# Issuing the first loads of a hybrid attention and mixture kernel from SyncE, and taking a maximum over partitions on TensorE and VectorE

## The chip, the cores and the metric

The kernel runs on one core of one Trainium2 chip. The metric is the device time of one execution in microseconds; lower is better. The engines are named PE (TensorE), DVE (VectorE), ACT (ScalarE), POOL (GpSimd) and SP (SyncE).

## The reference

The input x has the shape [2, 2048, 256], 4096 tokens of 256 float32 values, and passes four residual blocks: linear attention, a mixture-of-experts FFN, causal softmax attention, and the same FFN again.

```python
x = x + attn_a(_layernorm(x), Wqkv, Wout, bout)
x = x + ffn(_layernorm(x), ln_gamma, ..., gens, gc_w, gc_b)
x = x + attn_b(_layernorm(x), Wq, bq, Wk, bk, Wv, bv, Wo, bo)
x = x + ffn(_layernorm(x), ln_gamma, ..., gens, gc_w, gc_b)
```

In the FFN the output of the experts is multiplied by three matrix exponentials before it is mixed with a dense branch:

```python
for i in range(NROT):                  # NROT = 3
    moe_out = moe_out @ expm(gens[i])  # gens: [3, 256, 256]
```

Only weights go into the exponentials, so the kernel computes them once, before it touches x, and folds their product into the experts' second weights.

## The kernel before, in words

`build` calls five stages one after the other: `weights()`, `context()` (linear attention), `mixture(0)`, `attention()` and `mixture(1)`. A stage is one block, in which each engine has its own instruction stream; streams meet only through semaphores, and at the end of a block all engines meet at a barrier. The order on each engine is the order in which the code is written.

The change lies in `weights()`, L185 to L536, which works on three matrices of 256x256 in float32 (NROT = 3, each as two chunks of 128 partitions):

- **ScalarE** (L407) first issues the load of the generators (L409, semaphore `w_gens`), then the four projection matrices of the softmax attention (L411), x in four pieces of 1 MB (L414), and the small weights of the linear attention (L416 to L419). Only then comes its compute: the copies of PE's transposes out of the PSUM banks (L422, recorded as L163, since the helper `copy` stands there).
- **SyncE** (L226) issues 14 small loads (L241 to L245, semaphore `w_small`), waits for `w_gens`, and issues the experts' weights: `ew1` in two pieces of 2 MB (L248) and `ew2` in four of 1 MB (L251). Last it writes a blank tile (L255).
- **GpSimd** (L258) builds constants (iotas, identity, masks, zeros), then waits for `g_mx` and takes the maximum over all 128 partitions with `partition_all_reduce` (L306, semaphore `g_all`).
- **VectorE** (L308) sums the absolute values of each generator row (L338), takes the maximum per partition (L340, signals `g_mx`), waits for `g_all`, works out from the maximum how many squarings are needed and the scale (L342 to L348), and scales the generators (L350, signals `A_ok`).
- **TensorE** (L448) waits for the identity and for `A_ok`, transposes each scaled matrix (L454, inside the helper `transposed`), and forms powers of it with `product` (L462) from the transposes that ScalarE has copied. VectorE copies the squares out (L355), builds polynomials (L359, L362), and finishes Horner's scheme (L377). A hardware loop then squares the results (L384), two products join the three exponentials (L387, L389), and the stage ends with small products that need the experts' weights (L508, which waits for `w_ew`) and the projections (L516, `w_proj`), and with splits into bfloat16 parts on VectorE (L322 to L327).

`context()` starts behind the barrier. There SP issues nothing at first, GpSimd fills a row with ones (L648) and then takes inverse square roots with the operation `pow` for each group of tokens (L579, in `roots`), VectorE takes statistics of x (L561 to L572), waits for the root, and normalises (L680); PE's first work in this stage is the transpose of the first normalised group (L788), and all its other work of the stage stands behind it.

Of the kernel before, what the change touches and what calls it, by code (L numbers as in the profile page):

```python
# [18 lines left out]
ACT, ALU, AX = mybir.ActivationFunctionType, mybir.AluOpType, mybir.AxisListType  # L19
P = 128  # L20
# [5 lines left out]
def build(nc, d, out):  # L26
    B, N, C = d["L0_attn_a_x"].shape
    HD = d["L0_attn_a_Wout"].shape[0]
# [5 lines left out]
    NT = T // P  # L34
# [13 lines left out]
    with ctx:  # L48
# [5 lines left out]
        def sem(name):  # L54
            taken.append(nc.alloc_semaphore(name))
            return taken[-1]
# [15 lines left out]
        xs = sb("xs", [P, NT, C])  # L72
        keys = under("keys", [P, 2, KC, N], F32)
        rows = under("rows", [P, 2, 2, (KC + HC) * P], F32)
# [19 lines left out]
        ident = sb("ident", [P, P])  # L94
# [74 lines left out]
        def weights():  # L169
# [23 lines left out]
            gsum = a2.take(NROT * KC)  # L193
            gmx, gall = a2.take(1), a2.take(1)
            thr = a2.take(24)
# [12 lines left out]
            dve = sem("dve_order")  # L208
            g_mx, g_all, A_ok, AT_ps, AT_ok = sem("g_mx"), sem("g_all"), sem("A_ok"), sem("AT_ps"), sem("AT_ok")
            horner_ps, X_ok, s_ok = sem("horner_ps"), sem("X_ok"), sem("s_ok")  # L210
# [14 lines left out]
            with nc.Block() as block:  # L225
                @block.sync  # L226
                def _(sp):
# [17 lines left out]
                    sp.dma_start(gcb[:], d["L0_ffn_gc_b"].partition_broadcast(P)).then_inc(w_small, 16)  # L245
                    sp.wait_ge(w_gens, 16)
                    for c in range(KC):
                        sp.dma_start(ew1[:, c, :, :], d["L0_ffn_ew1"][:, c * P:(c + 1) * P, :].rearrange("e p h -> p e h")  # L248
                                     ).then_inc(w_ew, 16)
# [9 lines left out]
                def _(pool):  # L259
                    n = 0  # L260

                    def then(ins):
                        nonlocal n
                        n += 1
                        ins.then_inc(order, 1)
                        pool.wait_ge(order, n)

                    def select(t, pattern, base, cm, op, fill):
                        return pool.affine_select(out=t, in_=t, compare_op=op, fill=fill, base=base, pattern=pattern,
                                                  channel_multiplier=cm)  # L270
# [8 lines left out]
                    then(pool.memset(ident[:], 0.0))  # L279
                    select(ident[:], [[-1, P]], 0, 1, ALU.not_equal, 1.0).then_inc(consts, 1)  # L280
                    then(pool.memset(eye, 0.0))
                    select(eye, [[P, KC], [-1, C]], 0, 1, ALU.not_equal, 1.0).then_inc(consts, 1)
# [16 lines left out]
                    pool.memset(onesb[:], 1.0).then_inc(consts, 1)  # L299
                    pool.memset(onesf[:], 1.0).then_inc(consts, 1)  # L300
                    pool.memset(mhalf[:], -0.5).then_inc(consts, 1)
                    for t in (eb1p, eb2p, abbp, vbp):
                        pool.memset(t[:], 0.0).then_inc(consts, 1)

                    pool.wait_ge(g_mx, 1)
                    pool.partition_all_reduce(gall, gmx, P, bass.bass_isa.ReduceOp.max).then_inc(g_all, 1)  # L306

                @block.vector  # L308
                def _(v):
                    n = 0  # L310

                    def then(ins):

                        nonlocal n
                        n += 1
                        ins.then_inc(dve, 1)
                        v.wait_ge(dve, n)

                    def parts(o, src, width, rows):
# [19 lines left out]
                                         apply_absolute_value=True))  # L339
                    v.tensor_reduce(gmx, gsum, AX.X, ALU.max).then_inc(g_mx, 1)  # L340
                    v.wait_ge(g_all, 1)
                    then(v.tensor_scalar(cmp, thr, gall, None, ALU.is_lt))  # L342
                    then(v.tensor_reduce(sf, cmp, AX.X, ALU.add))
# [7 lines left out]
                    v.wait_ge(A_ok, NROT)  # L351
                    v.wait_ge(consts, 2)
                    for m in range(NROT):
# [54 lines left out]
                def _(act):  # L408
                    act.dma_start(gens, d["L0_ffn_gens"].rearrange("m (c p) j -> p m c j", p=P)).then_inc(w_gens, 16)  # L409
                    for o, k in zip(w4, "qkvo"):  # L410
                        act.dma_start(o, d[f"L0_attn_b_W{k}"].rearrange("(c p) n -> p c n", p=P)).then_inc(w_proj, 16)  # L411
                    for q in range(4):
                        ts = slice(q * NT // 4, (q + 1) * NT // 4)
                        act.dma_start(xs[:, ts, :], d["L0_attn_a_x"].rearrange("b (n p) c -> p (b n) c", p=P)[:, ts, :]  # L414
                                      ).then_inc(x_in, 16)
                    act.dma_start(wqkv, d["L0_attn_a_Wqkv"].rearrange("(c p) n -> p c n", p=P)).then_inc(x_in, 16)  # L416
                    act.dma_start(wout[:], d["L0_attn_a_Wout"]).then_inc(x_in, 16)
                    for b in range(B):
                        act.dma_start(ctxm[HD:HD + 1, b, :], d["L0_attn_a_bout"].rearrange("(o n) -> o n", o=1)).then_inc(x_in, 16)  # L419
                    for m in range(NROT):  # L420
# [28 lines left out]
                def _(pe):  # L449
# [15 lines left out]

                    pe.wait_ge(consts, 1)
                    for m in range(NROT):
# [1267 lines left out]
```

## Time and profile before

| what | value |
|---|---|
| median of 3 runs | 1540.83 us (1539.09 to 1541.23) |
| the profiled execution | 1532.49 us |
| its span, first to last instruction | 1530.9 us |
| mean granted TensorE clock | 0.885 of full speed |
| busy share PE / DVE / ACT / POOL | 78% / 50% / 37% / 27% |
| `weights()`, to the first instruction of `context()` | 0 to 140.1 us |

A row of the timeline gives the start in us from the start of the span, the duration, the engine, the line, the operation, what is written and read, and the count where equal instructions were merged; in brackets stands the idle time of the engine ahead of it and what ended that time. ACTq, SPq and POOLq are the engines' instruction queues, where DMA issues and configuration instructions are recorded. "issue" as a releaser means that the engine waited for nothing that the profile shows. Clock is a share of full speed: 1.00 is 2.4 GHz and 0.50 is 1.2 GHz.

### The profile page before, as it was taken

What the parts mean: (1) busy time and instruction counts of PE and PEld (TensorE: products, weight loads), DVE (VectorE), ACT (ScalarE), POOL (GpSimd) and SP (SyncE); (2) the same over time, 40 slices, a digit from 0 to 9 for tenths busy, and PEclk for the clock granted to TensorE, in tenths of its full rate; (3) what the DMA queues carried; (4) which work ended last, traced back from release to release, by engine and by line L of the source; (5) the groups of instructions that cost most, each with busy time, mean ns of one, the idle gap of its engine ahead of it and who ended that gap; (6) DMA issues with size and microseconds to landing.
All of it is one profiled execution on the core that took longest, in us unless ns stands there. A gap on an engine that the chain in (4) does not pass through costs nothing. (4 is left out here: it accounts for less than half of the span.)

```text
span 1530.9 us, 26055 instructions
## 1 busy us (share of the span) xinstructions
PE 1200.2 (78%) x7496; PEld 1008.5 (66%) x7497; DVE 761.7 (50%) x2430; ACT 573.2 (37%) x1143; POOL 412.3 (27%) x479
## 2 busy tenths in 40 slices
PE   1895886991899999930789968998881899999940
PEld 1772664871788888830679856897770778888830
DVE  1624674885334444448644455444775234444438
ACT  0110553440444444445333223332440344444435
POOL 2001110477243443410100010000576244443410
PEclk8998897696899999975899989999785999999975
DMA  9200233267633333343000000000266743333346
GB/s 317 86 0 0 83 124 124 90 204 231 221 120 98 100 94 96 97 164 109 1 0 1 1 1 0 1 1 1 111 221 230 250 136 96 122 98 93 97 170 220
DMA packets 75432, 161.12 MB, mean 105 GB/s; under 512 B 11270, under 2 KB 36562, under 8 KB 75354
## 3 DMA queue, kind: packets, MB, share of 16 engines
q1 hardware_dynamic: 49190, 99.42, 18.8%
q0 software_dynamic: 19776, 54.45, 11.6%
q10 hardware_dynamic: 6388, 6.29, 1.3%
q8 instruction: 38, 0.62, 0.2%
q14 instruction: 40, 0.33, 0.1%
HBM read 88.66 MB, written 71.47 MB: 105 GB/s over the span
## 5 line engine op out<-in xcount | busy, mean ns | idle before, releaser
L1397 PE MATMUL bank<-ew,rows 128*128 x852 | 298.5, 350 | 5.9 <-DVE rows L1076 3.0
L1399 PE MATMUL bank<-ew,rows 128*128 x852 | 274.1, 322 | 0.0
L1398 PE MATMUL bank<-low_in,rows 128*128 x852 | 273.7, 321 | 0.0
L1189 POOL DMA_INDIRECT results<-xh x142 | 141.8, 999 | 353.5 <-DVE xh L1059 209.6
L1076 DVE TENSOR_TENSOR rows<-bank,rows 128x512 fp32r<-128x512 f32 x142 | 98.3, 692 | 217.8 <-ACT rows L163 217.8
L1397 PEld LDWEIGHTS bank<-ew,rows 128*128 128x128 f32 x852 | 162.2, 190 | 14.9 <-issue 8.0
L1399 PEld LDWEIGHTS bank<-ew,rows 128*128 128x128 f32 x852 | 162.7, 191 | 12.6
L1398 PEld LDWEIGHTS bank<-low_in,rows 128*128 128x128 f32 x852 | 163.6, 192 | 6.8
L163 ACT ACTIVATE rows<-bank 128x256 fp32r<-128x256 f32 (+1 forms) x284 | 138.8, 489 | 69.1 <-PE bank L1405 66.9
L579 POOL TENSOR_TENSOR work<-work,mhalf 128x8 f32<-128x8 f32 (+1 forms) x20 | 37.9, 1894 | 450.5 <-DVE work L572 450.4
L163 ACT ACTIVATE xh<-bank 128x256 f32<-128x256 f32 (+1 forms) x181 | 76.4, 430 | 196.1 <-PE bank L1431 139.1
L1282 ACT ACTIVATE xh<-bank 128x512 f32<-128x512 f32 x142 | 84.9, 598 | 153.2 <-PE bank L1416 153.2
L1169 POOL DMA_INDIRECT slots_in<-xh,work x128 | 126.9, 992 | 51.4 <-issue 36.0
L1052 DVE TENSOR_TENSOR rows<-bank,rows 128x256 fp32r<-128x256 f32 x142 | 60.3, 425 | 153.9 <-ACT rows L163 153.0
L1330 PE MATMUL bank<-abw,work 128*128 128x256 f32 (+1 forms) x512 | 113.0, 356 | 4.4 <-ACT ab L1264 2.4
L1613 PE MATMUL bank<-values,shares 128*128 128x256 f32 x816 | 111.8, 288 | 2.0 <-DVE shares L1541 1.9
L1613 PE MATMUL bank<-keys,queries 128*128 128x512 f32 (+2 forms) x480 | 107.9, 379 | 4.8 <-issue 4.8
L1405 PE MATMUL bank<-ident,xh 128*128 128x128 f32 x284 | 56.1, 279 | 69.1 <-DMA xh<-slots_in 68.9
L1613 PEld LDWEIGHTS bank<-values,shares 128*128 128x128 f32 x816 | 101.3, 190 | 3.5 <-DVE shares L1541 3.2
L1330 PEld LDWEIGHTS bank<-abw,work 128*128 128x128 f32 x512 | 88.5, 222 | 21.0 <-ACT ab L1264 5.1
L1613 PEld LDWEIGHTS bank<-keys,queries 128*128 128x128 f32 x480 | 86.2, 197 | 18.5 <-issue 5.2
L1405 PEld LDWEIGHTS bank<-ident,xh 128*128 128x128 f32 x284 | 40.1, 145 | 81.5 <-issue 63.2
(285 smaller groups left out, 2068.6 us busy)
## 6 DMA issues: line engine op xcount, KB each, us to landing
xh<-slots_in POOLq DMA_DIRECT2D x142, 129.0 KB, 2.5
xh<-results SPq DMA_DIRECT2D x16, 1032.0 KB, 5.5
low_in<-low SPq DMA_DIRECT2D x32, 512.0 KB, 4.5
residual<-xs SPq DMA_DIRECT2D x16, 512.0 KB, 5.8
dense<-ab SPq DMA_DIRECT2D x16, 512.0 KB, 5.8
xs<-residual SPq DMA_DIRECT2D x16, 512.0 KB, 4.5
ab<-dense SPq DMA_DIRECT2D x16, 512.0 KB, 5.4
xs<-in_L_attn_a_x_dram ACTq DMA_DIRECT2D x4, 1024.0 KB
```

The costliest lines, as they stand in the source:

```text
L163: return eng.activation(o, i, ACT.Copy, scale=scale)
L1052: v.tensor_tensor(f32r(q[:, 1]), bank[:, k % 2, 0:C], q[:, 0], ALU.subtract).then_inc(xrT_ok, 1)
L1076: v.tensor_tensor(f32r(q[:, 1]), bank[:, 4 + k % 2, :], q[:, 0], ALU.subtract).then_inc(hidT_ok, 1)
L1169: pool.indirect_dma_start(out=xg, out_offset=bass.IndirectOffsetOnAxis(ap=slot[:, k, t:t + 1], axis=0), in_=xh[:, t, :], in_offset=None).t ...
L1189: pool.indirect_dma_start(out=yg, out_offset=bass.IndirectOffsetOnAxis(ap=back[j % RING], axis=0), in_=yr[j % RING], in_offset=None).then_ ...
L1282: act.activation(hid[k % 2], bank[:, 2 + k % 2, :], ACT.Gelu).then_inc(hid_ok, 1)
L1330: pe.matmul(o, xT[g % 2][:, c, t * P:(t + 1) * P], abw[:, c, some], start=(c == 0), stop=False)
L1397: pe.matmul(o, hi, f32r(high(c)), start=(c == 0), stop=False)
L1398: pe.matmul(o, hi, f32r(low(c)), start=False, stop=False)
L1399: pe.matmul(o, lo, f32r(high(c)), start=False, stop=False)
L1405: last = pe.transpose(bank[:, k % 2, c * P:(c + 1) * P], xr[k % RING][:, c * P:(c + 1) * P], ident[:])
L1613: last = pe.matmul(o, f32r(left(x)), f32r(right(y)), start=(start and q == 0), stop=(stop and q == 2), skip_group_check=True)
```

## The change

ScalarE keeps only the load of the generators. The loads of x, of the small weights of the linear attention and of the four projections move to SyncE, in this order, between its wait for `w_gens` and the loads of the experts' weights. The maximum over partitions goes another way: PE transposes the column of 128 partial maxima into one row of PSUM bank 7, VectorE reduces that row, PE multiplies a row of ones with the result so that it stands in all 128 partitions, and VectorE copies it out. GpSimd writes the row of ones (`onesf`) earlier, right behind the identity, and no longer runs `partition_all_reduce`.

```diff
 @block.sync
     sp.wait_ge(w_gens, 16)
+    for q in range(4):
+        ts = slice(q * NT // 4, (q + 1) * NT // 4)
+        sp.dma_start(xs[:, ts, :], d["L0_attn_a_x"].rearrange("b (n p) c -> p (b n) c", p=P)[:, ts, :]
+                     ).then_inc(x_in, 16)
+    sp.dma_start(wqkv, d["L0_attn_a_Wqkv"].rearrange("(c p) n -> p c n", p=P)).then_inc(x_in, 16)
+    sp.dma_start(wout[:], d["L0_attn_a_Wout"]).then_inc(x_in, 16)
+    for b in range(B):
+        sp.dma_start(ctxm[HD:HD + 1, b, :], d["L0_attn_a_bout"].rearrange("(o n) -> o n", o=1)).then_inc(x_in, 16)
+    for o, k in zip(w4, "qkvo"):
+        sp.dma_start(o, d[f"L0_attn_b_W{k}"].rearrange("(c p) n -> p c n", p=P)).then_inc(w_proj, 16)
     for c in range(KC):
         sp.dma_start(ew1[:, c, :, :], ...
 @block.gpsimd
     select(ident[:], [[-1, P]], 0, 1, ALU.not_equal, 1.0).then_inc(consts, 1)
+    pool.memset(onesf[:], 1.0).then_inc(consts, 1)
...
     pool.memset(onesb[:], 1.0).then_inc(consts, 1)
-    pool.memset(onesf[:], 1.0).then_inc(consts, 1)
...
-    pool.wait_ge(g_mx, 1)
-    pool.partition_all_reduce(gall, gmx, P, bass.bass_isa.ReduceOp.max).then_inc(g_all, 1)
 @block.vector
     v.tensor_reduce(gmx, gsum, AX.X, ALU.max).then_inc(g_mx, 1)
+    v.wait_ge(g_row, 1)
+    v.tensor_reduce(gtop, bank[0:1, 7, 0:P], AX.X, ALU.max).then_inc(g_top, 1)
     v.wait_ge(g_all, 1)
+    then(v.tensor_copy(gall, bank[:, 7, P:P + 1]))
     then(v.tensor_scalar(cmp, thr, gall, None, ALU.is_lt))
...
-    v.wait_ge(consts, 2)
+    v.wait_ge(consts, 3)
 @block.scalar
     act.dma_start(gens, d["L0_ffn_gens"].rearrange("m (c p) j -> p m c j", p=P)).then_inc(w_gens, 16)
-    for o, k in zip(w4, "qkvo"):
-        act.dma_start(o, d[f"L0_attn_b_W{k}"].rearrange("(c p) n -> p c n", p=P)).then_inc(w_proj, 16)
-    for q in range(4):
...
-    act.dma_start(wqkv, d["L0_attn_a_Wqkv"].rearrange("(c p) n -> p c n", p=P)).then_inc(x_in, 16)
-    act.dma_start(wout[:], d["L0_attn_a_Wout"]).then_inc(x_in, 16)
...
 @block.tensor
-    pe.wait_ge(consts, 1)
+    pe.wait_ge(consts, 2)
+    pe.wait_ge(g_mx, 1)
+    pe.transpose(bank[0:1, 7, 0:P], gmx, ident[:]).then_inc(g_row, 1)
+    pe.wait_ge(g_top, 1)
+    pe.matmul(bank[:, 7, P:P + 1], onesf[:], gtop, start=True, stop=True).then_inc(g_all, 1)
     for m in range(NROT):
         pe.wait_ge(A_ok, m + 1)
```

How the instructions of GpSimd stand before, from the end of `weights()` over the start of `context()`. The rows "ISA" without a tile are recorded in the trace as MODIFY_POOL_CONFIG, the row "ISA work<-work" is the reduction over partitions, and the TENSOR_TENSOR rows of L579 are the `pow`:

```order
L303 MEMSET vbp 65x256
L306 ISA
L306 ISA work<-work 128x1 [waits g_mx]
L225 UNCONDITIONAL_BRANCH
L646 UNCONDITIONAL_BRANCH [waits barrier_Pool_Activation_PE_DVE_SP_gather]
L648 MEMSET work 1x4096
L579 ISA
L579 TENSOR_TENSOR ab<-ab,mhalf 128x8 [waits a_arg,a_ones]
L579 TENSOR_TENSOR ab<-ab,mhalf 128x8 [waits a_arg] x7
```

The same place of the change, where the line numbers are higher by 4 in `context()`:

```order
L650 UNCONDITIONAL_BRANCH [waits barrier_Pool_Activation_PE_DVE_SP_gather]
L652 MEMSET work 1x4096
L583 TENSOR_TENSOR ab<-ab,mhalf 128x8 [waits a_arg,a_ones]
L583 TENSOR_TENSOR ab<-ab,mhalf 128x8 [waits a_arg] x7
L630 UNCONDITIONAL_BRANCH
```

The reduction has gone with the configuration instruction ahead of it, and so has the configuration instruction ahead of the first `pow`. One at the program's start (L272, now L282) remains.

SyncE in the change, from its wait for the generators to its last store of the stage:

```order
L249 DMA xs<-in_L_attn_a_x_dram 128x8x256 [waits w_gens]
L249 DMA xs<-in_L_attn_a_x_dram 128x8x256 x3
L251 DMA ab<-in_L_attn_a_Wqkv_dram 128x2x192
L252 DMA wout<-in_L_attn_a_Wout_dram 64x256
L254 DMA ctxm<-in_L_attn_a_bout_dram 1x256 x2
L256 DMA ab<-in_L_attn_b_Wq_dram 128x2x256
L256 DMA ab<-in_L_attn_b_Wk_dram 128x2x256
L256 DMA ab<-in_L_attn_b_Wv_dram 128x2x256
L256 DMA ab<-in_L_attn_b_Wo_dram 128x2x256
L258 DMA ew<-in_L_ffn_ew_dram 128x8x512 x2
L261 DMA ew<-in_L_ffn_ew_dram 128x8x256 x4
L265 DMA slots_in<-zero 128x258 [waits zero_ok]
```

Before, the wait for `w_gens` stood directly at the loads of `ew`; now twelve loads stand between. On ScalarE this is what remains ahead of its copies:

```order
L417 UNCONDITIONAL_BRANCH [waits barrier_Pool_Activation_PE_DVE_SP_release]
L419 DMA xh<-in_L_ffn_gens_dram 128x6x256
L163 ACT_TABLE_LOAD
L163 ACTIVATE xh<-bank 128x512 [waits AT_ps] x3
L163 ACTIVATE ab<-bank 128x512 [waits A3_ps] x3
```

The table load stands directly behind the one DMA, and only the copy behind it waits for PE.

## Rows read from the trace of the kernel before

**Rows 1.** Page, first line.

```profile
span 1530.9 us, 26055 instructions
```

**Rows 2.** Timeline from 0 us: the path from the generators to ScalarE's first copies.

```profile
6.22 1.75 DVE L338 TENSOR_REDUCE work<-xh 128x6 f32<-128x1536 f32 x1 [2.99 <-DMA xh<-in_L_ffn_gens_dram]
...
8.01 0.16 DVE L340 TENSOR_REDUCE work<-work 128x1 f32<-128x6 f32 x1
...
18.91 12.05 ACTq L416 DMA_DIRECT2D ab<-in_L_attn_a_Wqkv_dram  x1
20.13 0.38 POOL L306 PARTITION_ALL_REDUCE work<-work  x1 [6.96 <-issue]
20.55 0.24 DVE L342 TENSOR_SCALAR work<-work 128x24 f32<-128x24 f32 x1 [12.38 <-POOL work L306]
...
22.48 2.79 PE L454 MATMUL bank<-ident,xh 128*128 128x128 f32 x12 [22.48 <-DVE xh L350]
...
33.39 1.28 ACT L163 ACT_TABLE_LOAD   x1 [33.39 <-issue]
34.68 1.57 ACT L163 ACTIVATE xh<-bank 128x512 f32<-128x512 f32 x3
...
39.25 0.69 DVE L355 COPY xh<-bank 128x512 f32<-128x512 f32 x1 [16.12 <-PE bank L462]
40.89 0.69 DVE L355 COPY xh<-bank 128x512 f32<-128x512 f32 x1 [0.95 <-PE bank L462]
```

**Rows 3.** Timeline of PE alone, the first products.

```profile
35.33 12.43 PE L462 MATMUL bank<-xh 128*128 128x256 f32 x48 [10.06 <-ACT xh L163]
```

**Rows 4.** Configuration instructions of GpSimd, lines L306 and L579.

```profile
L306 POOLq MODIFY_POOL_CONFIG  x2: 1/1/1, 13.1 to 13.2; - x2
L579 POOLq MODIFY_POOL_CONFIG  x2: 1/1/1, 143.7 to 143.7; - x2
```

**Rows 5.** Timeline at the start of `context()`.

```profile
140.13 3.50 POOL L648 MEMSET work<- 1x4096 f32 x1 [119.62 <-POOLq L225]
...
142.42 1.25 DVE L572 TENSOR_SCALAR ab<-ab 128x4 f32<-128x4 f32 x1
150.46 1.68 POOL L579 TENSOR_TENSOR ab<-ab,mhalf 128x8 f32<-128x8 f32 x1 [6.82 <-issue]
```

**Rows 6.** Single lines, durations in ns (min/median/max): the nearest to the four new instructions.

```profile
L454 PE MATMUL bank<-ident,xh x12: 421/422/447, 22.5 to 24.9; 128*128 128x128 f32 x12
L524 PE MATMUL bank<-work,ab x8: 250/250/272, 133.4 to 134.2; 128*128 128x1 f32 x8
L697 DVE TENSOR_REDUCE ab<-bank x8: 411/418/426, 169.7 to 244.5; 128x32 f32<-128x256 f32 x8
L402 DVE TENSOR_SCALAR qbias<-bank x1: 159/159/159, 137.1 to 137.1; 128x2 f32<-128x2 f32 x1
```

**Rows 7.** Windows: us, busy PE PEld DVE ACT POOL (instructions), clock, DMA share, GB/s.

```profile
38.00:39.00 1.00, 1.00 (x4) 0.76 (x3) 0.00 (x0) 0.00 (x0) 0.00 (x0) 0.50 1.10 344
39.00:40.00 1.00, 1.00 (x6) 0.90 (x5) 0.69 (x1) 0.00 (x0) 0.00 (x0) 0.99 1.11 330
...
59.00:60.00 1.00, 0.90 (x3) 0.82 (x4) 1.00 (x2) 0.00 (x0) 0.00 (x0) 0.75 0.39 132
...
60.00:100.00 40.00, 40.00 (x206) 34.84 (x206) 12.60 (x19) 8.00 (x15) 0.00 (x0) 0.96 0.00 0
```

**Rows 8.** Timeline: SyncE's loads of the experts' weights, and PE's first use.

```profile
8.30 2.60 SPq L248 DMA_DIRECT2D ew<-in_L_ffn_ew_dram  x2
...
10.93 28.25 SPq L251 DMA_DIRECT2D ew<-in_L_ffn_ew_dram  x4
...
112.67 13.90 PE L508 MATMUL bank<-ew,work 128*8 128x512 f32 x32
```

**Rows 9.** DMA issues: size of each, and median us from issue to landing.

```profile
xh<-in_L_ffn_gens_dram ACTq DMA_DIRECT2D x1, 768.0 KB, 5.2
...
ab<-in_L_attn_b_Wo_dram ACTq DMA_DIRECT2D x1, 256.0 KB, 9.0
```

More of the change, by code:

```diff
@@ L193, in weights @@
             gsum = a2.take(NROT * KC)
-            gmx, gall = a2.take(1), a2.take(1)
+            gmx, gall, gtop = a2.take(1), a2.take(1), a2.take(1, rows=1)
             thr = a2.take(24)
@@ L208, in weights @@
             dve = sem("dve_order")
-            g_mx, g_all, A_ok, AT_ps, AT_ok = sem("g_mx"), sem("g_all"), sem("A_ok"), sem("AT_ps"), sem("AT_ok")
+            g_mx, g_row, g_top, g_all, A_ok, AT_ps, AT_ok = sem("g_mx"), sem("g_row"), sem("g_top"), sem("g_all"), sem("A_ok"), sem("AT_ps"), sem("AT_ok")
             horner_ps, X_ok, s_ok = sem("horner_ps"), sem("X_ok"), sem("s_ok")
@@ L409, in _ @@
                     act.dma_start(gens, d["L0_ffn_gens"].rearrange("m (c p) j -> p m c j", p=P)).then_inc(w_gens, 16)
-                    for o, k in zip(w4, "qkvo"):
-                        act.dma_start(o, d[f"L0_attn_b_W{k}"].rearrange("(c p) n -> p c n", p=P)).then_inc(w_proj, 16)
-                    for q in range(4):
-                        ts = slice(q * NT // 4, (q + 1) * NT // 4)
-                        act.dma_start(xs[:, ts, :], d["L0_attn_a_x"].rearrange("b (n p) c -> p (b n) c", p=P)[:, ts, :]
-                                      ).then_inc(x_in, 16)
-                    act.dma_start(wqkv, d["L0_attn_a_Wqkv"].rearrange("(c p) n -> p c n", p=P)).then_inc(x_in, 16)
-                    act.dma_start(wout[:], d["L0_attn_a_Wout"]).then_inc(x_in, 16)
-                    for b in range(B):
-                        act.dma_start(ctxm[HD:HD + 1, b, :], d["L0_attn_a_bout"].rearrange("(o n) -> o n", o=1)).then_inc(x_in, 16)
                     for m in range(NROT):
```

## The prediction

> **What bounds the kernel now.** I read the page first, then the timeline of the first 140 us, then the windows for the clock and the DMAs. The span is 1530.9 us [rows 1], and the change touches only `weights()`. It matters there because every stage ends at a barrier: what `weights()` takes is added to all that follows, whatever the engines' shares of busy time are.
>
> The reader is to see three waits. The first is on GpSimd. VectorE has its partial maxima at 8.17 us (8.01 + 0.16), but the reduction over partitions starts only at 20.13, after 6.96 us in which GpSimd waits for nothing the profile shows, and VectorE goes on at 20.55, after 12.38 us of idleness [rows 2]. The configuration instruction for that reduction stands at 13.1 to 13.2 [rows 4], so the order is: masks until 13.17, configuration, 6.96 us, 0.38 us of work.
>
> The second is on ScalarE. PE transposes the three matrices from 22.48 to 25.27 [rows 2], then idles for 10.06 us until ScalarE has copied the first one [rows 3]. ScalarE did not wait for PE: its queue was issuing loads until 33.39 (the one of the Wqkv weights alone held it for 12.05 us), and only then come the table load of 1.28 us and the first copy at 34.68 [rows 2]. The engines' DMA share is above 1.0 there and they move 330 to 344 GB/s [rows 7], so the issues are held up by full queues, and ScalarE's compute stands behind them.
>
> The third is in the next stage. GpSimd's fill ends at 143.63 and VectorE's argument is ready at 143.67 (142.42 + 1.25), yet the first `pow` starts at 150.46, after 6.82 us of "issue" [rows 5]. A configuration instruction stands at 143.7 here too [rows 4]. Since PE's first transposes of `context()` wait for this root, all of the stage waits with it.
>
> **Part 1, the maximum over partitions.** Removed: everything between 8.17 and 20.55, 12.38 us. Added: four small instructions in a chain with a handover between any two.
> - PE's transpose of one column, 128 columns moving: 0.42 us, as the first transposes of the stage took, which ran on a cold PE [rows 6].
> - VectorE's maximum of 1x128 from PSUM: no row has the shape. A 128x256 reduction from PSUM took 0.42, a 128x2 operation from PSUM 0.16 [rows 6]; half way in size, I take 0.30.
> - PE's product with one column: 0.25 from the products of 128x1 [rows 6]; doubled at half clock it would be 0.50.
> - VectorE's copy of 128x1 from PSUM: 0.16 from the 128x2 operation [rows 6].
> - Four handovers and one wait of VectorE for itself, at 0.04 each as between 20.13 + 0.38 and 20.55 [rows 2]: 0.20.
>
> Together 1.33 us, so L342 starts at 9.50 instead of 20.55: **11.05 us** earlier. The longest handover in these rows to PE is the 0.64 us from the start of L350, 21.84, to PE's start, and that holds an instruction of 0.43; two steps on PE that were each worse by 0.6 would cost 1.2, and I keep 9.8 as the low end. The row of ones is early enough: behind the identity its fill is done before 4 us, and the second matrix of constants is still waited for, by a count of three now, far ahead of its use.
>
> **A rule that speaks against this part.** The row shows 0.38 us for the reduction on GpSimd, less than my 1.33 us for the detour [rows 2]. The Trainium skill, GPSIMD Engine Reference, section "4.1 Engine selection", gives GPSIMD as the engine for a reduction along the partition dimension; by that rule alone the sum of this part would be a loss of 0.95 us, that is 1.33 less 0.38. The same page, "2.1 Instruction dispatch", says that the first call of a freshly loaded kernel pays about 6 us more with no visible instruction; the trace agrees, with 6.96 and 6.82 us.
>
> **Part 2, ScalarE freed.** With one DMA ahead, the table load runs from about 1.5 us, in the shadow of the generators' load. PE's transposes then run from 22.48 - 11.05 = 11.43 to 14.22 at the old pace. The first is done after a third of the 2.79 us, at 12.36, and ScalarE's first copy, about 0.6 us, ends at 13.0, before PE has finished transposing. So PE goes straight into its products at 14.22: the idle 10.06 us are gone, **10.06 us**, and nothing replaces them.
>
> **Part 3, the clock.** The first product of eight matmuls took from 35.33 to 39.2, the next 1.64 us (39.25 to 40.89) [rows 2, 3]. Clock was 0.50 until 39.0 and 1.00 from there [rows 7]; PE had then worked for 3.7 us, coming from idleness. In the change PE works unbroken from 11.43. If the clock rises 3.7 us from there, at 15.1, the first product has 0.9 us at half pace and ends 2.2 us after its start, not 3.9: a gain of 1.7. If it rises 3.7 us behind the products' start, the gain is 0. I take **1.0 us**.
>
> **Part 4, the generators' load.** Alone on ScalarE's queue it no longer shares the DMA engines with four projections. It took 5.2 us for 768 KB [rows 9]; at 330 GB/s [rows 7] the bytes alone are 2.4 us of that, and a fixed part that no row gives apart is the rest. Three of the four shared loads were issued by the time its bytes flowed, so I bound the gain by 0 and 0.7 and take **0.3 us**.
>
> **Part 5, the next stage.** The change has no configuration instruction left ahead of `pow`, only the one at the program's start. With it goes the wait: `pow` starts when the argument is ready, 143.7 instead of 150.46 in old time: **6.75 us**. This edit is in no line of the diff; it follows from the order of instructions on GpSimd.
>
> **What moves at no cost.** Twelve more loads on SyncE stand behind its wait for the generators. That wait costs nothing new: the small issues keep SyncE busy until 8.3 [rows 8], later than the generators land (6.2). Behind it come 13.9 MB (x 4096 KB, Wqkv, wout and projections 1280, `ew1` and `ew2` 8192). After 33.4 us ScalarE issues nothing, and the engines still move 330 to 344 GB/s from SyncE's queue [rows 7], so one queue fills them. At 330 the last byte lands at 8.3 + 42 = 50 us. The experts' weights are first used at 112.67 [rows 8], or 90 in the change: 40 us of cover. The biases and norm weights on SyncE's queue are wanted by VectorE after 58 us, now after 35; they are issued as before by 8.3, and the slowest of the loads beside them took 9.0 us [rows 9]. x is wanted at 117 at the earliest. The blank tile of SyncE, ahead of the barrier, is issued behind the last load, by about 46, also long before the barrier. If this cover were gone, each us by which the weights came after 90 would be lost.
>
> Behind the first products the chain of PE, VectorE and ScalarE moves as a whole: from 60 to 100 us PE was busy all 40 us with no DMA at all [rows 7]. One term may change: around 59.5 us, in the gap before PE's start at 59.1, the clock fell (0.75 over 59 to 60), and its mean of 0.96 from 60 to 100 says that it stayed at 0.50 for 3.2 us of those 40 [rows 7], at a cost of about 1.7 us. Whether it falls again when all stands 22 us earlier, and when it rises at the start of `context()`, is open: between -2 and +2 us, taken as 0.
>
> **Sum.** 11.05 + 10.06 + 1.0 + 0.3 + 6.75 = 29.2 us. The profiled execution took 1532.49 us, 1.6 beyond its span, and would take 1503.3. The median of the runs is 1540.83, 8.3 above the profiled one; I see no reason for the gain to scale and subtract it from the median: **1511.7 us**.
>
> **Rivals.**
> - *`pow` still waits for its code* at its first use, since what the start of the program configured is not resident by then. For it: 6.82 us are seen at that place, and no row shows a `pow` without a change of configuration ahead of it. Against: both waits follow such an instruction, and iotas and masks run at once at the start. Gain 22.4, time 1518.4. Chance 12%.
> - *One queue feeds the engines less well than two*, and PE waits for the experts' weights. At 330 GB/s there is no wait; at 140, the 13.9 MB take 99 us and end at 107.6, which is 17.5 too late: gain 11.7, time 1529. The Trainium skill, Perfetto Trace Analysis, "DMA Optimizations", advises balancing DMAs over the engines that can issue them where descriptor generation is the bottleneck, which speaks for this rival; the rows speak against its condition. Chance 2%.
> - *The same mechanism, slower than before*: it decides from below 125 GB/s, where the loads end after 8.3 + 111 = 119.4, the old 112.67 plus the 6.75 of part 5. At 110 GB/s they end at 134.7, 15.2 us past that: 1556. The nearest rows are three times faster. Chance 1%.
> - *ScalarE is not what PE waits for*: if the copies needed a first-use wait of their own of some 10 us, part 2 would fall and the gain be 19, time 1522. The table load in the rows is followed at once by the copy. Chance 3%.
>
> **How the numbers follow.** The forecast's case has 82%. Its own range adds the ends: at best 11.05 + 10.06 + 1.7 + 0.7 + 6.75 + 2 = 32.3, time 1508.5, and 1.5 more if the timed runs scatter as before (1539.1 to 1541.2); at worst 9.8 + 10.06 + 0 + 0 + 6.75 - 2 = 24.6, time 1516.2. The first rival lies at 1518.4 and is to be held for the most part, so the range is 1507 to 1520. A change under 0.2%, 3 us, could not be told from none here: faster 0.98, same 0.01, slower 0.01.
>
> **What would show it.** Right: L352 (the old L342) near 9.5 us, ScalarE's first copy near 12.4 and no idle time of PE ahead of L462; the first `pow` directly behind the fill of 4096 ones; the barrier of `weights()` near 118 us; DMAs finished by 55 us. Wrong: an "issue" wait of 6 us or more ahead of the first `pow` (the first rival), idle time of PE on a DMA ahead of L512 (the queue rivals), or a table load that starts late. The prediction fails as a whole if later stages, which have no edit, run longer by what was won.

## The result, and the profile after

| what | before | the change |
|---|---|---|
| median of 4 runs | 1541.03 us (1539.09 to 1542.66) | 1514.57 us (1512.38 to 1517.63) |
| the profiled execution | 1532.49 us | 1512.38 us |
| its span | 1530.9 us | 1510.8 us |
| first instruction of `context()` | 140.13 us | 119.47 us |
| first `pow` | 150.46 us | 123.19 us |

The ratio is 0.9847 (95% interval 0.9822 to 0.9871): the change is 26.5 us faster by the medians, where 29.2 were forecast. At the first `pow` it is 27.3 us ahead, at the first slot load of `mixture(0)` (the load of a tile of sorted tokens) 25.7, at the end of the profiled pair only 20.1; what is given back has a part of its own below.

The path to ScalarE's first copies, in the timeline of the change. Its columns are those explained ahead of the prediction, and the rows answer to [rows 2, 3]:

```profile
1.49 1.28 ACT L163 ACT_TABLE_LOAD   x1 [1.49 <-PEq L1728]
...
6.34 1.75 DVE L345 TENSOR_REDUCE work<-xh 128x6 f32<-128x1536 f32 x1 [3.22 <-DMA xh<-in_L_ffn_gens_dram]
...
6.92 3.55 POOL L279 TENSOR_SCALAR_AFFINE_SELECT sel<-sel 72x1024 bf16<-72x1024 bf16 x3
...
8.43 0.37 PE L468 MATMUL bank<-ident,work 128*1 128x128 f32 x1 [8.43 <-DVE work L347]
8.84 0.28 DVE L349 TENSOR_REDUCE work<-bank 1x1 f32<-1x128 f32 x1 [0.56 <-PE bank L468]
...
9.17 0.58 PE L470 MATMUL bank<-work,onesf 1*128 1x1 f32 x2 [0.37 <-DVE work L349]
9.79 0.16 DVE L351 COPY work<-bank 128x1 f32<-128x1 f32 x1 [0.68 <-PE bank L470]
9.99 0.52 DVE L352 TENSOR_SCALAR work<-work 128x24 f32<-128x24 f32 x1
...
11.56 1.92 DVE L360 TENSOR_SCALAR xh<-xh,work 128x512 f32<-128x512 f32 x3
...
12.47 2.82 PE L454 MATMUL bank<-ident,xh 128*128 128x128 f32 x12 [2.72 <-DVE xh L360]
...
15.09 12.01 PE L462 MATMUL bank<-xh 128*128 128x256 f32 x48
...
18.60 0.69 DVE L365 COPY xh<-bank 128x512 f32<-128x512 f32 x1 [5.11 <-PE bank L462]
```

The table load lies at the start, the four new instructions take the place of the reduction, and there is no bracket behind PE's products at 15.09: PE does not wait for ScalarE any more. The first copy out of the products stood at 39.25 before and stands at 18.60 now, 20.65 us earlier, and the whole stage keeps that: `context()` starts 20.66 us earlier. The start of `context()` on GpSimd, which answers to [rows 5]:

```profile
119.47 3.50 POOL L652 MEMSET work<- 1x4096 f32 x1 [105.74 <-POOLq L225]
...
121.69 1.32 DVE L575 TENSOR_SCALAR ab<-ab 128x4 f32<-128x4 f32 x1
121.77 1.25 DVE L576 TENSOR_SCALAR ab<-ab 128x4 f32<-128x4 f32 x1
123.19 1.67 POOL L583 TENSOR_TENSOR ab<-ab,mhalf 128x8 f32<-128x8 f32 x1 [0.21 <-DVE ab L576]
```

The `pow` now waits 0.21 us for VectorE instead of 6.82 us for nothing visible. VectorE's two TENSOR_SCALAR rows ahead of it end with GpSimd's fill, as the last section takes up. One queue feeds the DMA engines: in windows of 5 us of the change (columns as in [rows 7]) they move 334 to 387 GB/s from 15 us until the loads are done at about 50 us, 42 us ahead of the first use of the experts' weights at 92.01.

```profile
30.00:35.00 5.00, 3.72 (x18) 2.93 (x16) 5.00 (x9) 0.00 (x0) 0.00 (x0) 1.00 1.05 387
...
45.00:50.00 5.00, 5.00 (x25) 4.41 (x24) 2.08 (x3) 0.00 (x0) 0.00 (x0) 1.00 1.04 334
50.00:55.00 5.00, 5.00 (x30) 4.39 (x29) 1.38 (x2) 1.60 (x3) 0.00 (x0) 1.00 0.06 19
```

### The profile page after: what moved, and what is told of

Read it like the earlier page. It is cut to its first block and busy times, and to the rows that moved or that the text cites. A ratio compares the mean times of both kernels' runs of the same rounds, so it can differ in the third digit from the quotient of the medians.

```text
span 1510.8 us, 26058 instructions
## 1 busy us (share of the span) xinstructions
PE 1204.3 (80%) x7499; PEld 1010.8 (67%) x7500; DVE 763.9 (51%) x2432; ACT 573.7 (38%) x1143; POOL 412.8 (27%) x478
```

## The experiments

Theory: three waits went, two of them in series on one path (GpSimd's reduction, then ScalarE's queue of issues) and one in the next stage (the configuration ahead of `pow`). Rivals: ScalarE was not what PE waited for; `pow` waits at its first use whatever stands ahead; and what the profiled pair gives back later belongs to the loads on SyncE's queue. The diffs below are taken against the change.

**The kernel before once more.** No edit; a second profile.

> The kernel before, unchanged, for a second profile. In the first pair of profiles the change was 27.3 us ahead at the first pow of context(), still 25.7 at the first slot load of mixture(0), and only 20.4 at the end of that mixture. Theory A (scatter): the start of the expert tiles in mixture(0), where slot loads, scatters and low weights share the DMA engines, varies from run to run by about 5 us whatever the kernel; this second profile of before then has the same weights() (first instruction of context() at 140.1, first pow at 150.5, within 0.3) and reaches the first gather of results later than the first profile did, since the runs of before have a median 8 us over that profile: span about 1535 to 1540. Theory B (given back by a mechanism of the change): the profile of before repeats to 1 us, span about 1531, and the difference in mixture(0) belongs to the change.

Measured: 1540.45 us, ratio 1.0001 (0.9984 to 1.0017), span 1537.8. `context()` starts at 140.9 and the first slot load of `mixture(0)` stands at 383.6, as in the first profile within 1 us, but the span is 7 us longer. So the first profile of before was a short execution, and a difference of two spans is known to no better than that. What is called the stretch from here on, from the first slot load to the last scatter of results in `mixture(0)`, took 286.6 us (285.4 in the first profile). That is not the cause of the difference, so this did not decide between A and B. The wait of GpSimd ahead of the reduction was 5.95 us here, 6.96 in the first profile.

**The loads alone.** The maximum is taken on GpSimd again; the loads are where the change has them.

```diff
 @block.gpsimd
+    pool.wait_ge(g_mx, 1)
+    pool.partition_all_reduce(gall, gmx, P, bass.bass_isa.ReduceOp.max).then_inc(g_all, 1)
 @block.vector
-    v.wait_ge(g_row, 1)
-    v.tensor_reduce(gtop, bank[0:1, 7, 0:P], AX.X, ALU.max).then_inc(g_top, 1)
     v.wait_ge(g_all, 1)
-    then(v.tensor_copy(gall, bank[:, 7, P:P + 1]))
 @block.tensor
-    pe.wait_ge(g_mx, 1)
-    pe.transpose(bank[0:1, 7, 0:P], gmx, ident[:]).then_inc(g_row, 1)
-    pe.wait_ge(g_top, 1)
-    pe.matmul(bank[:, 7, P:P + 1], onesf[:], gtop, start=True, stop=True).then_inc(g_all, 1)
```

> The change of the loads alone; the maximum is taken on GpSimd as before. Own theory: the reduction still starts at about 20.1 behind 7 us of loading code, PE's transposes at about 22.5, and its products follow at 25.1 without idle time: weights() ends at about 129.5 to 130 instead of 140.1, and the first pow still waits 6.8 us behind the fill. Time 10 to 11 us below before, about 1530.5. Rival (ScalarE was not what PE waited for): PE idles ahead of its products as before, no gain. Rival (the clock makes up the difference): since PE's idle time is gone, the first product takes 2.2 instead of 3.9 us, and the gain is 11.8.

Measured: 1529.49 us, ratio 0.9928 (0.9911 to 0.9945), 11.1 us faster by the ratio. The timeline of this kernel, the same path, and its first `pow`:

```profile
19.25 0.38 POOL L316 PARTITION_ALL_REDUCE work<-work  x1 [6.06 <-issue]
...
21.59 2.79 PE L454 MATMUL bank<-ident,xh 128*128 128x128 f32 x12 [21.59 <-DVE xh L360]
...
24.18 11.41 PE L462 MATMUL bank<-xh 128*128 128x256 f32 x48
...
27.09 0.69 DVE L365 COPY xh<-bank 128x512 f32<-128x512 f32 x1 [4.85 <-PE bank L462]
```

```profile
127.71 3.50 POOL L648 MEMSET work<- 1x4096 f32 x1 [108.09 <-POOLq L225]
138.32 1.68 POOL L579 TENSOR_TENSOR ab<-ab,mhalf 128x8 f32<-128x8 f32 x1 [7.10 <-issue]
```

PE goes straight from its transposes into its products, as the theory has it, and `context()` starts 12.4 us earlier: 0.9 from a shorter wait of GpSimd (6.06 us), 10.3 from the idle time, 1.0 from the first product, which took 2.9 us instead of 3.9. The expectation was 10 to 10.6; the shorter wait, which varies as much between profiles of before, and the product make up the rest. The rival that ScalarE was not what PE waited for falls. `pow` waits 7.10 us here.

**The maximum alone.** ScalarE issues all its loads ahead of its copies, as before.

```diff
 @block.scalar
     act.dma_start(gens, ...).then_inc(w_gens, 16)
+    for o, k in zip(w4, "qkvo"):
+        act.dma_start(o, ...).then_inc(w_proj, 16)
...
 @block.sync
     sp.wait_ge(w_gens, 16)
-    for q in range(4):
-        ts = slice(q * NT // 4, (q + 1) * NT // 4)
...
```

> The change of the maximum alone; ScalarE issues all its loads as before. Own theory: PE's transposes are done by 16, but the first copy still stands at 34.7, so weights() ends at 140.1 as before; only the wait ahead of the first pow is gone, 6.6 us. Time about 1534.5. Rival (pow waits at its first use whatever stands ahead of it, and in the change something else hid this): no gain, 1541. Together with the loads alone this says that the two edits are not additive: each alone gives 10 to 11 and 0 in weights(), both give 20.6.

Measured: 1534.84 us, ratio 0.9964 (0.9951 to 0.9977), 5.5 us faster by the ratio. In its timeline PE is ready 10 us earlier and waits 10 us longer:

```profile
12.48 2.82 PE L454 MATMUL bank<-ident,xh 128*128 128x128 f32 x12 [2.98 <-DVE xh L350]
...
34.89 5.29 PE L462 MATMUL bank<-xh 128*128 128x256 f32 x15 [19.59 <-ACT xh L163]
...
139.68 3.50 POOL L652 MEMSET work<- 1x4096 f32 x1 [125.94 <-POOLq L225]
143.39 1.67 POOL L583 TENSOR_TENSOR ab<-ab,mhalf 128x8 f32<-128x8 f32 x1 [0.21 <-DVE ab L576]
```

`weights()` ends 0.4 us earlier, less than the 1.5 us by which the three profiles of before differ there (139.4 to 140.9), so nothing is to be told from that. The gain is the wait ahead of `pow`, gone with the configuration instruction. So in `weights()` the loads alone give 12.4 us, the maximum alone 0.4, and both 20.7: the second wait hid the first.

**A reduction that nobody reads.** The change, with the reduction beside the path, into a tile of its own.

```diff
 @block.gpsimd
+    pool.wait_ge(g_mx, 1)
+    pool.partition_all_reduce(gidle, gmx, P, bass.bass_isa.ReduceOp.max)
```

> The whole change, with partition_all_reduce put back on GpSimd beside it, its result going into a tile that nobody reads. Own theory: the reduction is off the path and costs nothing in weights() (context() starts at 119.5), but a configuration instruction stands ahead of the first pow again, and pow waits 6.8 us: 6.6 us slower than the change, about 1521. Rival (the wait has to do with the long path before, not with the change of configuration): as the change, 1514.6.

Measured: 1520.59 us, ratio 0.9869 (0.9846 to 0.9891): by the medians 6.0 us slower than the change, as expected, by the ratios 3.4, and their intervals overlap. The trace decides. The start of `context()` and the configuration in this kernel:

```profile
119.41 3.50 POOL L656 MEMSET work<- 1x4096 f32 x1 [98.86 <-POOLq L226]
129.96 1.68 POOL L587 TENSOR_TENSOR ab<-ab,mhalf 128x8 f32<-128x8 f32 x1 [7.05 <-issue]
```

```profile
L587 POOLq MODIFY_POOL_CONFIG  x2: 1/1/1, 122.9 to 123.0; - x2
```

`context()` starts as in the change (119.41), and the first `pow` 6.77 us later than there. In the code nothing else differs, so the wait belongs to the reduction and the configuration instruction that it leaves ahead of `pow`; the two were not taken apart. Using one `partition_all_reduce` costs 6 to 7 us twice, ahead of it (5.95 to 6.96 us in the five profiles with it) and ahead of the next `pow` (6.82 to 7.10). The rival that `pow` waits at its first use whatever stands ahead falls.

**The change once more.** No edit.

> The change, unchanged, for a second profile. In the profiles so far, the stretch from the first slot load of mixture(0) to its last scatter of results took 285.4 and 286.6 us in before, 287.9 with the maximum alone, but 289.7 in the change, 291.0 with the loads alone and 290.8 with the unused reduction: the three kernels with the loads on SyncE lose 3 to 5 us there, nearly all of it within the first seven tiles (43.0 to 43.8 against 47.0 to 47.8 us to the eighth scatter). Theory B (belongs to the loads on SyncE's queue): 289.5 to 291 again, 47 to 48 to the eighth scatter. Theory A (scatter of runs, three against three by chance): 285 to 291, anywhere.

This chip gave longer times for every kernel, the kernel before included (1577.42 us): from the first scatter of slots to the first slot load the change took 116.2 us here and 97.2 in its first profile. In `mixture(0)` PE waited 19.6 us for ScalarE's gelu (1.1 in the first profile), in the whole execution 42.3 us (2.4). The ratio to before is 0.9829 (0.9805 to 0.9853), 26.7 us by the medians. The stretch took 287.4 us, with 43.9 to the seventh scatter, the one that the expectation counts as the eighth: against theory B, on this chip.

**The loads late on ScalarE.** The change, with the moved loads back on ScalarE, behind its copies of the powers.

```diff
 @block.scalar
         act.wait_ge(A3T_ps, m + 1)
         copy(act, AT[:, m], ...).then_inc(A3T_ok, 1)
+    for o, k in zip(w4, "qkvo"):
+        act.dma_start(o, ...).then_inc(w_proj, 16)
...
```

> The change, but the moved loads go back to ScalarE's queue, behind its nine copies of the powers instead of ahead of them, so SyncE's queue carries what it did before. Theory B (the state or filling of SyncE's queue is what slows the first tiles of mixture(0)): that stretch is back to 285 to 288 us, 43 to 44 us to the eighth scatter, while context() still starts at 119.5: 3 to 4 us faster than the change, about 1511. Theory A (scatter): no difference to the change but for chance, 1514.6. If the late issue holds ScalarE back at the squaring (its next copy is at 51.2, its copies end at 29.2, and 5.5 MB are 16 us at 340 GB/s behind SyncE's 8.4 MB), context() starts later by what it overruns, at most a few us.

Measured on the same chip as the run above: 1552.20 us, ratio 0.9840 (0.9815 to 0.9866); `context()` starts at 120.0, the stretch took 287.1 us. No difference to the change can be told, in time or in the stretch, where theory B expected 3 to 4 us. That also shows that what helped is *when* ScalarE issues, not which engine does: with 5.5 MB on its queue behind the copies nothing is lost that these runs could show.

**Horner's scheme interleaved.** In the change one wait of PE is left in this part (timeline of PE of the change):

```profile
28.28 5.44 PE L462 MATMUL bank<-xh 128*128 128x256 f32 x24
38.44 11.85 PE L462 MATMUL bank<-xh 128*128 128x256 f32 x46 [4.72 <-DVE xh L387]
```

```diff
-for q, i in enumerate((3, 2, 1, 0)):
-    (both steps of polynomial i, for all m)
+poly(0, 3)
+for q, i in enumerate((2, 1, 0)):
+    poly(q + 1, i)
     v.wait_ge(b_ok, NROT * (q + 1))
     for m in range(NROT):
         v.wait_ge(horner_ps, NROT * q + m + 1)
         v.scalar_tensor_tensor(X[:, m], ...).then_inc(X_ok, 1)
```

> The change, with VectorE's polynomials built one at a time between the steps of Horner's scheme instead of all four ahead of them. In the change PE waits 4.7 us for VectorE at 38.4 and then runs 48 products, some of them at half clock. Own theory: the path through the first stage was handed to VectorE's polynomials (14.5 us) when ScalarE and GpSimd went off it; interleaved, PE has products to do meanwhile, its wait shrinks to about 1 us at a time and the clock does not fall: context() starts 5 to 6 us earlier, at about 114; time about 1509. Rival (VectorE and PE now alternate and each step waits for the other): no gain, 1514.6.

Measured on the same chip as the two above: 1544.38 us, ratio 0.9789 (0.9762 to 0.9815), 6.3 us below the change there. PE works without a gap, and the windows from 36 to 44 us show clock 1.00 throughout:

```profile
27.93 16.07 PE L464 MATMUL bank<-xh 128*128 128x256 f32 x72
44.03 1.85 PE L456 MATMUL bank<-ident,xh 128*128 128x128 f32 x12
```

`context()` starts at 113.2 instead of 119.3: 6.1 us.

**Before and the change on one chip.** No edits; these two and the two below ran on a third chip.

> The kernel before, for one more profile beside the next one on the same chip. Question: does the stretch of mixture(0) from the first slot load to the last scatter belong to the kernel or to chance? So far before: 285.4, 286.6 (first chip or chips). Theory A (chance, or the chip): this one and the next lie within 285 to 291 with no order between them. Theory B (the loads on SyncE slow it): this one is 3 us or more below the next.

> The change, for one more profile. Its stretch was 289.7 in the first profile and 287.4 in the second, on another chip. Theory A: no order against before on the same chip; with that the difference of the spans comes to what the first two stages win, 27.3 us, give or take the scatter of 3 to 5 us. Theory B: 3 us or more above before, and the difference of the spans is 20 to 24.

Measured: before 1538.54 us (beside 1540.42 for its other runs, ratio 0.9991), the change 1510.93 us, ratio 0.9805 (0.9772 to 0.9838), 29.5 us by the medians (27.6 against the run beside it). In this pair of profiles the change is 26.3 us ahead at the first `pow` (123.70 against 150.00) and 24.8 by the spans. The stretch took 287.0 and 286.7 us: no order between them.

**The fills moved.** The change, with two fills of GpSimd behind VectorE's urgent work.

```diff
 @block.gpsimd (weights)
+    pool.wait_ge(A_ok, NROT)
     pool.memset(onesb[:], 1.0).then_inc(consts, 1)
 @block.gpsimd (context)
-    pool.memset(work[HD:HD + 1, 0:T], 1.0).then_inc(ones_ok, 1)
-    pool.wait_ge(ones_ok, 1)
     for g in range(NG):
         nrm.roots(pool, g)
+    pool.wait_ge(nrm.root_ok, NG)
+    pool.memset(work[HD:HD + 1, 0:T], 1.0).then_inc(ones_ok, 1)
+    pool.wait_ge(ones_ok, 1)
```

> The change, with GpSimd's last six constants of weights() held back until the generators are scaled, and its fill of 4096 ones in context() behind all roots. In the change VectorE's three scalings took 1.92 us beside those fills and 1.28 before, and the arguments of the first pow took 1.3 us beside the fill of ones. Theory (the two engines hinder each other): scalings 1.28 again; from the start of context() to the first pow 2.6 instead of 3.7 us, 1.3 us in all, which the runs can hardly tell. Against it: the fill at the end lies ahead of the barrier; it ends before the stage does if the last root is taken 3.5 us before the end, as it was. Rival (those durations have another cause): no change in them.

Measured: 1513.25 us, ratio 0.9830 (0.9800 to 0.9860), no faster than the change. Its timeline at three places, and the times in ns of the four instructions of L686 near 193 us (least, median, most):

```profile
10.34 0.24 DVE L353 TENSOR_SCALAR work<-work 128x24 f32<-128x24 f32 x1
...
11.64 1.28 DVE L361 TENSOR_SCALAR xh<-xh,work 128x512 f32<-128x512 f32 x3
```

```profile
122.15 1.68 POOL L584 TENSOR_TENSOR ab<-ab,mhalf 128x8 f32<-128x8 f32 x1 [107.63 <-DVE ab L577]
```

```profile
192.73 0.16 DVE L681 SCALAR_TENSOR_TENSOR ab<-ab 128x4 f32<-128x4 f32 x1 [1.75 <-POOL ab L584]
192.76 3.51 POOL L656 MEMSET work<- 1x4096 f32 x1
192.93 4.44 DVE L686 TENSOR_SCALAR ab<-xs,ab 128x256 f32<-128x256 f32 x4
```

```profile
L686 DVE TENSOR_SCALAR ab<-xs,ab x4: 395/400/3481, 192.9 to 197.0; 128x256 f32<-128x256 f32 x4
```

The scalings are back at 1.28 us and the first `pow` comes 1.6 us earlier than in the change on this chip (123.70), as expected. But the fill now runs from 192.76 to 196.27, beside VectorE's normalisation, which takes 4.44 us; elsewhere four of them take 1.38. The single times show that this is no general slowing: the first of the four took 3.48 us, to 196.4, just behind the fill's end, and the others 0.40. VectorE's instruction was held until the fill was done. The same fill costs 1.1 us at the start of the stage and 3.1 at this place, while it keeps its own length (3.51 us against 3.50), and it was better off where it stood. PE then ran short of work, busy for 0.77 of the 4 us from 196, and the mean clock of the next 4 us was 0.57; the last `pow` of `context()` had come 3.7 us earlier than in the change on this chip (191.06 against 194.75), the first one of the next stage comes 0.4 us later (238.05 against 237.69). The step of the expectation that failed is that the fill would cost nothing because it ends before the stage does.

**Both together, and a last version.** The interleaved scheme with both fills moved, and then with only the six constants moved.

> The interleaved Horner scheme (6.1 us earlier at the start of context(), ratio 0.9789 against 0.9829 of the change) together with the fills moved back. If both hold: context() starts at 112.7 to 113, the first pow at 115.6; time 33 to 35 us below before, ratio about 0.978. If the fills give nothing: as the interleaved kernel, 32 to 33 us below.

> The interleaved Horner scheme with the six constants of weights() held back, but the fill of 4096 ones at the start of context() where the change has it. In the kernel with both fills moved the fill at the end ran beside VectorE's normalisation of the last group, which took 4.44 us there instead of 1.38, so 3 us were lost that the start had won in part. If the fill is what cost, this one keeps the 6 us of the interleaving: context() starts at 112.7 to 113.5, the first slot load of mixture(0) 6.5 to 8 us ahead of the change's 356.6 where the chip has no other delay, ratio to before about 0.977 to 0.979. If the interleaving's 6 us are given back later by something else, the ratio is 0.980 to 0.982 as with both fills moved.

Measured: both fills moved 1509.42 us, ratio 0.9795 (0.9766 to 0.9824), 31.0 us below before by the medians, under the 32 to 35 of the expectation, which its interval still covers; only the constants moved 1505.90 us, ratio 0.9777 (0.9756 to 0.9797), 34.5 us below before. That is the lowest median here, but its interval overlaps those of the other two interleaved kernels, so the runs do not rank the three. In the last one `context()` starts at 113.07, the first `pow` stands at 116.78, and the first slot load of `mixture(0)` at 347.3, 9.6 us ahead of the change's 356.9; the stretch behind it took 292.8 us against 289.7, which gives 3.1 of them back. The run with both fills moved shows the same held instruction as above (3.48 us).

Both kernels hold the constants back, as the run before did, but VectorE's L353 is not short in them. Their timelines in turn:

```profile
9.71 0.80 DVE L353 TENSOR_SCALAR work<-work 128x24 f32<-128x24 f32 x1
```

```profile
9.88 0.64 DVE L353 TENSOR_SCALAR work<-work 128x24 f32<-128x24 f32 x1
```

What decides there is the mask ahead of the constants, which no run moved; the next part comes back to it.

## Why the prediction was right, and where it was off

The time, 1514.57, lies in the range (1507 to 1520), 2.9 us above the forecast. By its steps, from the first profile of the change:

- **Part 1, 11.05 us forecast, 10.01 measured** (PE's transposes at 12.47 against 22.48). The detour from 8.28 to 9.99 took 1.71 us, not 1.33: the handovers from VectorE to PE took 0.15 and 0.05 us and the product with the row of ones 0.58 in two instructions instead of 0.25. But this term did not set the time. L352, behind the detour, took 0.52 us instead of 0.24 and ended at 10.51, just behind the end of GpSimd's mask at 10.47 (6.92 + 3.55). In the ten profiles with the detour it starts between 9.71 and 10.34. In eight it ends at 10.49 to 10.52, however early it started; in one, where it starts last, it takes its 0.24 us and ends at 10.58; in one the mask ends at 10.75 and it at 10.79. So it is held until the mask ends: at 10.51 instead of the forecast 9.74, 0.77 us that a shorter detour would not have won back. The other 0.27 us came behind it, where PE started 0.91 us after the start of the scalings instead of 0.64; the scalings took 1.92 us beside GpSimd's fills instead of 1.28, and 1.28 again in the three runs with those fills held back. The step that was mis-sized is VectorE's work, moved at its old length: a moved instruction meets other neighbours, and I had not asked which.

  By the rows this detour beats the reduction on GpSimd, against the rule of the Trainium skill's GPSIMD Engine Reference, "4.1 Engine selection", that the prediction weighed: 1.7 us of detour stand against 7.3 us of waiting and reducing, and 6.8 more in the next stage. The Trainium skill's sentence on the load of code, GPSIMD Engine Reference, "2.1 Instruction dispatch", agrees with the ten waits measured here, 5.95 to 7.10 us.
- **Part 2, 10.06 forecast, 10.23 measured** (from PE's transposes to its products 2.62 us, from 12.47 to 15.09; before 12.85, from 22.48 to 35.33). The loads alone confirm it by themselves.
- **Part 3, 1.0 forecast, 0.4 measured:** the first product took 3.51 us from 15.09 to 18.60, against 3.92. Its size varies from run to run: without the gap ahead of it the first product took 2.2 to 3.5 us in ten profiles, with the gap 3.6 to 3.9 in four. So a gain of 1.0 lies within what was seen, and 0.4 is one draw of it. Bounds 0 and 1.7 held.
- **Part 4, 0.3 forecast, nothing measured:** the generators' sum starts at 6.34 instead of 6.22. This 0.1 is within the 10.01 of part 1 and cost nothing, since the mask holds VectorE until 10.5 in any case; the sum started anywhere from 6.07 to 6.49 in nine of the profiles with the detour, and the instruction behind L352 stood at 10.52 to 10.55 in eight of them and at 10.81 in the one with the later mask. Leaving the queue to the generators gave nothing, and could have given nothing on this path.
- **Part 5, 6.75 forecast, 6.61 measured** (3.72 us from the start of the stage to `pow`, against 10.33), and its cause was shown by putting a reduction back.
- **What moves at no cost:** held. Loads end at 50 us as worked out, PE did not wait for them, and the queue rivals fall. The clock was at 0.50 behind PE's 4.7 us gap in both, 3.4 us long, from about 38.6 us in the change and 59.5 before, so the term taken as 0 was 0 in this pair. In both it fell just behind PE's new start (38.44 and 59.10), where the prediction puts it in the gap.

Together 27.3 us were won by the first `pow` in this pair, 1.9 less than the 29.2 forecast, and the three pairs of medians give 26.5, 29.5 and 26.7. So the mechanism was as forecast, and its sizes were off by 1.0 us in part 1, 0.6 in part 3 and 0.3 in part 4. The sum left out the scatter of later stages. In the first pair it took 7.2 us, of which 4.3 lie in the stretch and 1.6 between the first `pow` and the first slot load; in the pair of the third chip it took 1.5.

**What stays open.** In the first profile of the change the stretch in `mixture(0)` took 289.7 us. With the loads on SyncE it took 286.6 to 287.4 on two chips (five profiles), but 289.7 to 292.8 in four profiles on others; with the loads on ScalarE it took 285.4 to 287.9 in all five. On three chips both kinds ran side by side: on two the stretch was the same (287.0 against 286.6 and 286.7 us; 287.1 against 287.1 and 287.4), on the third it was 3 to 4 us longer with the loads on SyncE (291.0 and 290.8 against 286.6 and 287.9). In the longer ones the second scatter waits longer for the first to land, while low weights are loaded; a row of the change and the same place before:

```profile
379.31 1.00 POOL L1193 DMA_INDIRECT results<-xh  x1 [5.37 <-DMA results<-xh]
```

```profile
402.28 1.01 POOL L1189 DMA_INDIRECT results<-xh  x1 [2.71 <-DVE xh L1059]
```

Whether that is chance, the chip, or something of the queue that some chips show, is not settled.

## What to carry to other kernels

Ask of an engine that computes what its queue of DMA issues does while the DMA engines are full: 13 loads held ScalarE's first copy until 34.7 us, and twelve of them cost nothing that could be seen on SyncE, or on ScalarE behind the copies. Where two waits lie on one path, an edit alone may not show its worth (12.4 and 0.4 us against 20.7 together), so take both before judging either. Before you move an instruction of VectorE to an earlier time, look at what GpSimd does at that time: it may be held until GpSimd's instruction ends. And look at GpSimd for changes of configuration: one special operation is paid for twice, once ahead of it and once when ordinary work resumes, and the second bill can fall in a stage that the diff does not touch.

## What the runs showed of the hardware that was not expected

- A fill or a mask of GpSimd can hold an instruction of VectorE until it ends. Beside a fill of 3.51 us one TENSOR_SCALAR of 128x256 took 3.48 us and the three behind it 0.40 each; L352, 128x24, took 0.24 to 0.91 us, whatever was left until the mask's end. At the start of `context()` L575 and L576 took 1.32 and 1.25 us, to 123.01 and 123.02, where the fill ends at 122.97; without a fill beside them they take 0.17. VectorE's other operations beside that fill, BATCH_NORM_STATS2, TENSOR_TENSOR and SCALAR_TENSOR_TENSOR, kept their length (1.41 us for four, 0.16 to 0.17 for one).
- The recorded clock is no guide at the start of an execution: it reads 1.00 from 15 to 19 us in the change, while PE's first product took 3.51 us and the next 1.63, as the pair before did at a recorded 0.50 and 1.00.
- Chips differ by more than this change: the kernel before took 1577.42 us on one and 1539.94 to 1541.03 on the others. For the change, whose profiled execution was 36.9 us longer there, PE's wait for ScalarE's gelu in the two mixtures accounts for the most (42.3 us against 2.4). No profile of the kernel before was taken on that chip, and the cause is open.
